# Attention over batches: a flat ring of exponentials, two units in one GpSimd multiply, and the product with v six units behind

## What is computed

```python
def _L1_conv_ref(x, w_qkv, b_qkv):
    R = 32
    B, C, H, W = x.shape
    d = C // R
    HW = H * W
    xr = x.reshape(B, C, HW).transpose(0, 2, 1).reshape(B, HW, R, d).transpose(0, 2, 1, 3)
    qkv = jnp.einsum('brnd,ed->brne', xr, w_qkv) + b_qkv
    q, k, v = jnp.split(qkv, 3, axis=-1)
    attn = jnp.einsum('brnd,brmd->brnm', q, k)
    attn = jax.nn.softmax(attn, axis=0)
    out = jnp.einsum('brnm,brmd->brnd', attn, v)
    out = out.transpose(0, 2, 1, 3).reshape(B, HW, C).reshape(B, -1, H, W)
    return out
...
x = x + _L1_conv_ref(_gn(x), L1_conv_w_qkv, L1_conv_b_qkv)
```

## Time and profile before

| | us |
|---|---|
| median of 3 runs | 600.87 (597.69 to 601.31) |
| the profiled execution | 600.21 |
| its span, first to last instruction | 598.2 |
| from the first maximum to the end of the last sum | 297.8 |

### The profile page before, as it was taken

How to read it: one execution, slowest core, us unless ns; L and a number is a source line. 1 busy time by engine, 2 the same in 40 slices (tenths; PEclk the granted TensorE clock), 3 DMA queues, 4 the chain that set the end, 5 groups by cost and what they waited for, 6 DMA issues and landing times.

```text
span 598.2 us, 13058 instructions
## 1 busy us (share of the span) xinstructions
PE 504.8 (84%) x4610; PEld 308.1 (52%) x4611; DVE 481.1 (80%) x876; ACT 328.3 (55%) x709; POOL 387.7 (65%) x243
## 2 busy tenths in 40 slices
PE   3999687877877778777777877799999999999996
PEld 1554354444444444444444444468986656656665
DVE  5658967999999999999999999978777873333455
ACT  3624674676676766767667676624433533333341
POOL 3200483999899998999999899923105267766640
PEclk9998895999899999999999899999999999999999
DMA  7130257244243332332433320000013223322276
GB/s 225 37 110 1 85 167 253 81 124 130 78 112 84 94 105 73 112 98 80 106 88 93 96 78 2 2 1 1 2 55 101 71 75 107 99 87 90 83 290 211
DMA packets 34288, 56.62 MB, mean 95 GB/s; under 512 B 8541, under 2 KB 21494, under 8 KB 34102
## 3 DMA queue, kind: packets, MB, share of 16 engines
q1 hardware_dynamic: 28950, 43.95, 24.8%
q0 software_dynamic: 3744, 10.39, 5.6%
q10 hardware_dynamic: 1536, 1.51, 0.8%
HBM read 38.43 MB, written 17.40 MB: 93 GB/s over the span
## 4 chain that ended last, share of the span: by engine, by line
PE 37%; POOL 29%; DVE 17%; issue 10%; ACT 3%; DMA 3%; POOLq 0%; SPq 0%; ACTq 0%; DVEq 0%
POOL e_ring L459 29%; PE ps L1890 12%; PE ps L1911 6%; DVE m_bf L1042 4%; DVE x_hat L1049 4%; PE ps L1693 2%; PE ps L1820 2%; DVE stats L865 2%; PE ps L1879 2%; ACT e_ring L644 1%; PE ps L1900 1%; PE ps L1590 1%; PE ps L1621 1%; PE ps L1839 1%; PE ps L1767 1%
## 5 line engine op out<-in xcount | busy, mean ns | idle before, releaser
L459 POOL TENSOR_TENSOR e_ring<-e_ring,x_hat 128x1024 f32<-128x1024 f32 (+1 forms) x127 | 269.8, 2127 | 30.7 <-ACT x_hat L655 18.5
L644 ACT ACTIVATE e_ring<-ps 128x1024 f32<-128x1024 f32 x128 | 131.1, 1025 | 89.7 <-PE ps L1693 89.5
L1042 DVE TENSOR_REDUCE m_bf<-ps 128x128 bf16<-128x1024 f32 x128 | 154.9, 1211 | 4.2 <-PE ps L1684 4.2
L1049 DVE TENSOR_REDUCE x_hat<-e_ring 128x128 f32<-128x1024 f32 x128 | 154.5, 1207 | 3.2 <-ACT e_ring L644 3.2
L1693 PE MATMUL ps<-m_bf,ident_neg 128*128 128x512 bf16 x256 | 82.2, 404 | 61.7 <-DVE m_bf L1042 61.5
L1712 PE MATMUL ps<-e_ring,v_slot 128*32 128x128 f32 x2048 | 86.5, 286 | 1.1 <-POOL e_ring L459 0.6
L1684 PE MATMUL ps<-q_stack,k_stack 72*128 72x128 bf16 x1024 | 83.4, 227 | 3.9 <-DMA k_stack<-qk_parts 3.9
L1712 PEld LDWEIGHTS ps<-e_ring,v_slot 128*32 128x32 f32 x2048 | 50.4, 110 | 58.0 <-issue 51.1
L1684 PEld LDWEIGHTS ps<-q_stack,k_stack 72*128 72x128 bf16 x1024 | 61.9, 101 | 32.0 <-issue 25.8
L1890 PE MATMUL ps<-w_sb,e_ring 128*128 x156 | 74.0, 598 | 1.3 <-ACT e_ring L744 0.8
L477 POOL DMA_INDIRECT e_ring<-token_rows,slot_x x39 | 37.7, 966 | 43.2 <-DVE slot_y L1331 29.5
(11 more groups left out here) (237 smaller groups left out, 674.2 us busy)
## 6 DMA issues: line engine op xcount, KB each, us to landing
q_stack<-qk_parts SPq DMA_DIRECT2D x32, 288.0 KB
k_stack<-qk_parts SPq DMA_DIRECT2D x32, 288.0 KB
w_sb<-in_w13T_dram SPq DMA_DIRECT2D x16, 256.0 KB, 7.6
qk_parts<-e_ring SPq DMA_DIRECT2D x8, 384.0 KB, 3.4
qk_parts<-scratch SPq DMA_DIRECT2D x2, 1536.0 KB, 19.7
x_res<-in_x_dram SPq DMA_DIRECT2D x8, 256.0 KB, 3.9
w_sb<-in_w2T_dram SPq DMA_DIRECT2D x8, 256.0 KB, 7.5
work<-pair_rows SPq DMA_DIRECT2D x8, 256.0 KB, 4.7
```

What stands on the lines that cost most here:

```text
L459: nc.gpsimd.tensor_tensor(ev, ev, view(x_hat, CH + (u % RS) * P, [[0, quads], [1, P], [0, 2]]), ALU.mult).then_inc(norm_done, 1)
L644: nc.scalar.activation(e_ring[:, u % ER, :].rearrange("p (q n k) -> p q n k", q=BQ, k=2), view(ps, 2 * (v % SLOT) * CH, [[2 * P, BQ], [1, ...
L1042: nc.vector.tensor_reduce(m_bf[:, u % 2], view(ps, 2 * (v % SLOT) * CH, [[1, P], [P, B]]), AX, ALU.max).then_inc(max_done, 1)
L1049: nc.vector.tensor_reduce(s_sum[:, u % 2], by_position(e_ring[:, u % ER, :]), AXY, ALU.add).then_inc(sum_done, 1)
```

## The change

The exponentials are written batch by batch: a slot of the ring is 8 rows of 128 floats, as in PSUM. ScalarE reads and writes both in order. VectorE's sum takes, for each position, 8 floats that lie 128 floats apart, with one axis reduced instead of two. GpSimd multiplies two neighbouring slots of the ring in one instruction of 2048 floats, when the inverses of both units are there; only the half of unit 126 stays an instruction of its own. TensorE's product reads 128 floats in a row, and comes six units behind the scores instead of five, which also moves the copying out of bank 6, the fourth refill of v's slots and the addition to the residual by one step, and adds a step to the drain.

```diff
--- before.py
+++ after.py
@@ -9,7 +9,6 @@
                       out):
     fp32, bf16 = mybir.dt.float32, mybir.dt.bfloat16
     ALU, ACT, AX = mybir.AluOpType, mybir.ActivationFunctionType, mybir.AxisListType.X
-    AXY = mybir.AxisListType.XY
 
 
     B, C, SIDE = x.shape[0], x.shape[1], x.shape[2]
@@ -36,7 +35,7 @@
     UNITS = NG * UPG
     UW = B * P
     ER = 8
-    LAG = 5
+    LAG = 6
     RS = 4
     SLOT = 3
     BQ = B // 2
@@ -456,14 +455,20 @@
             def weights(U, u, quads=BQ):
                 pool.wait_ge(r_done, U + 1)
                 ev = e_ring[:, u % ER, 0:quads * 2 * P]
-                nc.gpsimd.tensor_tensor(ev, ev, view(x_hat, CH + (u % RS) * P, [[0, quads], [1, P], [0, 2]]), ALU.mult
+                nc.gpsimd.tensor_tensor(ev, ev, view(x_hat, CH + (u % RS) * P, [[0, 2 * quads], [1, P]]), ALU.mult
                                         ).then_inc(norm_done, 1)
 
+            def two_units(U, u):
+                pool.wait_ge(r_done, U + 2)
+                ev = e_ring[:, u % ER:u % ER + 2, :].rearrange("p a (b n) -> p a b n", b=B)
+                nc.gpsimd.tensor_tensor(ev, ev, view(x_hat, CH + (u % RS) * P, [[P, 2], [0, B], [1, P]]), ALU.mult
+                                        ).then_inc(norm_done, 2)
+
             with pool.Fori(0, NG - 1) as g:
-                for u in range(UPG):
-                    weights(g * UPG + u, u)
-            for u in range(UPG - 2):
-                weights((NG - 1) * UPG + u, u)
+                for u in range(0, UPG, 2):
+                    two_units(g * UPG + u, u)
+            for u in range(0, UPG - 2, 2):
+                two_units((NG - 1) * UPG + u, u)
             weights(UNITS - 2, UPG - 2, BQ // 2)
             for b in range(B):
                 pool.wait_ge(xhat_act, B * 2 + b + 1)
@@ -641,8 +646,7 @@
 
                     for s in range(2):
                         act.wait_ge(parts_out[s], 16 * NCH)
-                nc.scalar.activation(e_ring[:, u % ER, :].rearrange("p (q n k) -> p q n k", q=BQ, k=2),
-                                     view(ps, 2 * (v % SLOT) * CH, [[2 * P, BQ], [1, P], [P, 2]]), ACT.Exp).then_inc(exp_done, 1)
+                nc.scalar.activation(e_ring[:, u % ER, :], score_banks(v), ACT.Exp).then_inc(exp_done, 1)
 
             def logarithm(U, u):
                 act.wait_ge(sum_done, U + 1)
@@ -1031,10 +1035,6 @@
             for n in range(2, 2 * H * NCH):
                 qk_tile(n)
 
-            def by_position(ap):
-
-                return ap.rearrange("p (q n k) -> p n q k", q=BQ, k=2)
-
             def maximum(U, v, u):
                 dve.wait_ge(scores_done, U + 1)
                 if later_than(U, 2):
@@ -1046,12 +1046,12 @@
                 dve.wait_ge(exp_done, U + 1)
                 if later_than(U, 2):
                     dve.wait_ge(ln_done, U - 1)
-                nc.vector.tensor_reduce(s_sum[:, u % 2], by_position(e_ring[:, u % ER, :]), AXY, ALU.add).then_inc(sum_done, 1)
+                nc.vector.tensor_reduce(s_sum[:, u % 2], view(e_ring, (u % ER) * UW, [[1, P], [P, B]]), AX, ALU.add).then_inc(sum_done, 1)
 
             def normalise_last(U, first):
                 dve.wait_ge(r_done, U + 1)
                 ev = e_ring[:, U % ER, first * 2 * P:UW]
-                nc.vector.tensor_tensor(ev, ev, view(x_hat, CH + (U % RS) * P, [[0, BQ - first], [1, P], [0, 2]]), ALU.mult
+                nc.vector.tensor_tensor(ev, ev, view(x_hat, CH + (U % RS) * P, [[0, 2 * (BQ - first)], [1, P]]), ALU.mult
                                         ).then_inc(norm_last, 1)
 
             def add_last(half):
@@ -1711,7 +1711,7 @@
                 for b in range(B):
                     last = nc.tensor.matmul(ps[32 * (b % 4):32 * (b % 4) + 32, 6, (b // 4) * N + nh * P:(b // 4) * N + (nh + 1) * P],
                                             v_slot[:, b * H + mh, i, :],
-                                            view(e_ring, (u % ER) * UW + (b // 2) * (2 * P) + b % 2, [[2, P]]),
+                                            view(e_ring, (u % ER) * UW + b * P, [[1, P]]),
                                             start=(u == 0 and b < 4), stop=(u == UPG - 1), skip_group_check=True)
                 last.then_inc(pv_done, 1)
 
```

## The result

The changed kernel takes 693.3 us (median of 3 runs, 693.03 to 694.76) against 600.87: 1.156 times as long, 95% interval 1.150 to 1.163. It is slower, as forecast, by 92 us instead of 68, and within the range that was given. The profiled execution took 693.03 us, its span 691.1.

A forecast was written before the change was run, and what follows sets the result against it. VectorE's maximum and sum were taken to bound the attention stage. The sum's new order 63 us, TensorE's clock 4 and the stage's end 1 made 68 us on 600.2: 668 us, range 599 to 700.

The forecast's parts named there:

- my own mechanism: VectorE's sum slowed by its new reading order as L957's row shows: 668 us, range 648 to 685, chance 0.49.
- What binds: Attention stage: VectorE's maximum and sum set the pace, 2.257 us a unit; GpSimd's multiply only seems to bind.
- Two units in one instruction: GpSimd's multiply of 2048 elements: 4.08 to 4.61 us; the saved start and wait are worth nothing to the end.
- Lag and later start: GpSimd's pair starts at its second inverse, product six steps behind: 0.4 to 0.9 us left, no wait.
- Exponentials and product: ScalarE's exponentials stay at 1025 ns, and TensorE's product waits for VectorE anyway: both at nothing.
- The sum: VectorE's sum reading numbers 512 bytes apart in SBUF: 0.49 us more each, 63 us in all (51 to 75).
- The bound of 1.13 us more: Upper limit for VectorE's new sum: a jump takes no longer than two numbers, so at most twice 1.13 us.
- TensorE's clock: TensorE idling in the attention stage may keep its clock low, needing 2.81 us a unit: 8 us, half counted, 4.
- The end of the stage: Last multiplies and products of attention: the last product starts 0.7 to 1.3 us later, taken as 1 us.
- the sum would cost nothing: Rival: VectorE takes a new SBUF address each cycle, as from PSUM; 601 us (599 to 603), chance 0.27.
- The dear step: Rival: the sum's step costs all it can, 729 us at ScalarE's price or 746 at the upper bound; chance 0.14.
- GpSimd as the bound: Rival: the sum costs nothing and GpSimd's pair exceeds VectorE's mean of 4.65 us; 604 to 611 us, chance 0.07.

The follow-up runs named there:

- flat_multiply_alone: Kernel before, but GpSimd's multiply takes its second operand as 128 different numbers in a row instead of each twice; 604.23 us against 598.28, 1.010 times.
- rest_of_change: Changed kernel, but VectorE's sum reads two neighbours and then jumps 1024 bytes, as before the change; 603.65 us, 1.009 times the kernel before.
- price_by_length: Changed kernel with GpSimd multiplying 16 floats a unit, the sum's old order, and unused VectorE instructions of several lengths and steps ahead of sums; 664.41 us.
- the table: Changed kernel, but units sum with 16 different steps from 1 to 128 floats between the 8 numbers of an output; 687.09 us in one execution.
- sum_order_alone: Kernel before with one line changed: VectorE's sum reads 8 numbers 512 bytes apart, as in the changed kernel; 693.75 us, 1.157 times the kernel before.

## Why the prediction was right, and where it was off

The time, 693.3 us, lies inside the stated 599 to 700, but that range is wide, from no price at all up to 700, and the range that I gave to my own mechanism, 648 to 685, was missed by 8 us. Direction, engine and mechanism were right; the size of one term was not, and the width of the range made up for it. Two of the signs missed with it: I expected the sum at 1.6 to 1.8 us and 2.7 to 2.8 us from unit to unit, and it took 1.86 and 2.99.

*What binds.* Right. VectorE paced the stage before and paces it now. The 29% of the chain on GpSimd's multiply said only that its result was awaited last: GpSimd waits 103.9 us after, 1.65 for each pair, and the stage is longer by what the sum costs VectorE.

*Two units in one instruction.* 4.54 us, inside 4.08 to 4.61 and at its upper side, because of the operand's order, as `flat_multiply_alone` shows. The page that I quoted (the Trainium skill, "GPSIMD Engine Reference", performance versus the Vector engine) gave 4497 ns for an add of this length: the trace has 4536 for the multiply.

*Lag and later start.* Right: they cost the stage nothing (`rest_of_change` has the old length to the hundredth), and in the changed kernel TensorE's weight loads for the product wait for GpSimd 7 times, 5.6 us in all, against 10 times and 5.1 us before. *Exponentials and product* were right as well (1023 ns).

*The sum.* This is the step that failed, in size: I priced the new order at 0.49 us and it costs 0.73, some 94 us in 128 units, of which the stage saw 91.25 since VectorE's waits shrank by 2.9. The mechanism, the engine and the row were right. The error lies in reading and scaling the row: the price was a difference of 39 to 57 ns between 100 elements and a base of 257 ns interpolated from other instructions. L957's own pattern with step 1 has records of 0.24 us and with step 16 of 0.30; from start to start it is 0.17 and 0.23 (`price_by_length`). So the difference is some 60 ns, 0.61 an element instead of 0.48, and 10 ns of reading in 100 elements become 13 us over 128 sums of 1024. That is about half of what was missing. The rest lies between 100 elements and the sum itself: 0.68 at 800 elements, and 0.72 for the sum in the stage, where a step of 512 bytes is a little dearer than one of 64 (1.88 against 1.80). ScalarE's row, 0.98, was too dear for VectorE. The bound of 1.13 us more held except at a step of 96 bytes, which the kernel doesn't use; so the argument behind it, that a jump takes no longer than two numbers, does not hold for every step.

*TensorE's clock.* The granted clock in the stage fell from 0.96 to 0.74, as I feared, but I counted 4 us for it and the stage shows none: the unit's 2.99 us leave room for TensorE's 2.81 at its lower level, and VectorE's idle time fell. The clock does cost at the end, as the next rows show.

*The end of the stage.* 2.45 us instead of 1. Timeline of the kernel before there (two lines), then of the changed kernel:

```profile
389.08 1.13 PE L1637 MATMUL ps<-ones_sb 128*128 128x512 f32 x2
389.10 2.29 DVE L1054 TENSOR_TENSOR e_ring<-e_ring,x_hat 128x512 f32<-128x512 f32 x2
...
477.24 2.95 DVE L1054 TENSOR_TENSOR e_ring<-e_ring,x_hat 128x512 f32<-128x512 f32 x2
477.38 1.72 POOL L458 TENSOR_TENSOR e_ring<-e_ring,x_hat 128x512 f32<-128x512 f32 x1
477.57 1.08 PE L1712 MATMUL ps<-e_ring,v_slot 128*32 128x128 f32 x16 [1.42 <-POOL e_ring L464]
478.58 2.08 PE L1637 MATMUL ps<-ones_sb 128*128 128x512 f32 x2
480.59 2.09 PE L1712 MATMUL ps<-e_ring,v_slot 128*32 128x128 f32 x48
```

I had the late half of 126, but not the filler L1637 (products whose result nothing uses), which keeps its place in the step list while the products move past it: it takes 2.08 us, at a granted clock of 0.50 from 477.0 to 480.6 us, where it took 1.13 at 1.00, and three products wait behind it instead of two. From the end of VectorE's multiplies to the end of the last product it is 2.5 us now, 0.7 before. The other 0.7 us are VectorE's multiplies themselves, 2.95 us instead of 2.29.

*The rivals.* That the sum would cost nothing rested on the maximum, which reads PSUM at the same step for nothing; the table shows that this says nothing of SBUF. The dear step did not come in full: 0.72 ns an element is about halfway between my 0.48 and its 0.98. GpSimd as the bound did not come.

## What to carry to other kernels

Before a layout is changed for one engine, read it once from every engine that touches it, and look at the innermost steps on the engine that binds: here a tidy flat order took 8 bytes in a row away from a reduction and cost 65% of that instruction. A price taken from a short instruction should be scaled from the same instruction with and without the feature, by starts; a base from its neighbours was off by 16 ns here (257 against 241), in an effect of 60. And a chain of waits that runs through an engine with a short idle time at every step shows who is waited for last, not who sets the pace.

## What was not expected of the hardware

- VectorE's sum of 1024 floats from SBUF by step: free up to 8 bytes, 1.55 us at 12 bytes, 1.80 to 1.98 from 16 to 512 bytes, and 2.54 at 96 bytes; from PSUM, at 512 bytes, the maximum of 1024 floats took the same 1.13 as the stream from SBUF. The dearer 96 bytes stay unexplained.
- GpSimd's multiply of 1024 floats took 2.135 us with each number of the second operand used twice in a row and 2.40 with 128 different ones in a row.
- VectorE's two multiplies at the end of the stage, each with two operands in SBUF, took 2.02 us in `sum_order_alone`, where GpSimd's last multiply had ended before they began, 2.95 in the changed kernel, 4.54 in `rest_of_change`, where GpSimd's last pair ran until 1.8 us after their start, and 5.88 in `flat_multiply_alone`, where single multiplies ran until 4.2 us after it. The Trainium skill ("SBUF — State Buffer", who interferes with whom) has this: such an instruction contends with a GpSimd one that reads SBUF, and a reduction does not. Both agree with these rows: the sums changed by 0.02 us when GpSimd was all but idle.
